# Four of eleven down groups of an FP4 feed-forward layer: exact codes in two passes and a rescale on VectorE, in place of three passes

## The reference

```python
def _dequant_fp4(packed_i32, scales_f16, group_size):      # 8 codes in a word, one scale for 128 inputs of one output
    vals = _FP4_LUT[nib.astype(jnp.int32)].reshape(out_f, in_p * 8)
    s_full = jnp.repeat(scales_f16.astype(jnp.float32).T, group_size, axis=1)
    return vals * s_full
w_gu = _dequant_fp4(gate_up_packed, gate_up_scales, GROUP_SIZE)     # 2816 x 512
w_down = _dequant_fp4(down_packed, down_scales, GROUP_SIZE)         # 512 x 1408: 11 groups of 128 inputs
gate, up = (gate_up[..., :I], gate_up[..., I:])                     # gate_up = x @ w_gu.T, I = 1408
h = jax.nn.silu(gate) * up
y = jnp.einsum('bsi,hi->bsh', h, w_down)
rms = jnp.sqrt(jnp.mean(y * y, axis=-1, keepdims=True) + EPS)
return y / rms
x = _layernorm(x + _L0_ffn_ref(x, ...), axis=-1)                    # the last of three such lines
```

## Time and profile before

| | |
|---|---|
| runs | 532.00, 533.84, 530.71 us; median 532.0 us |
| the profiled execution | 532.28 us, its span 530.6 us |
| busy share of the span: PE, ACT, POOL, DVE | 95%, 75%, 72%, 70% |
| matmuls | 3612 |
| mean granted clock of TensorE | 0.988 |
| DMA | 40.6 MB, 77 GB/s |

### The profile page before, as it was taken

One profiled execution on the slowest core, in us unless ns is written; L12 is line 12 of the kernel. 1 busy time (PEld: TensorE's weight loads), 2 busy tenths in 40 slices (PEclk: granted clock), 3 DMA queues, 4 the chain that ended last, 5 costly groups with the idle time before them and its releaser, 6 DMA issues.

```text
span 530.6 us, 11816 instructions
## 1 busy us (share of the span) xinstructions
PE 504.4 (95%) x3612; PEld 372.5 (70%) x3612; DVE 370.9 (70%) x1161; ACT 400.5 (75%) x962; POOL 383.6 (72%) x449
## 2 busy tenths in 40 slices
PE   8998986999999999999999999999999999999992
PEld 6776775668876677667766776777677667776651
DVE  2876665898887677867777787778686876674223
ACT  4478864046999988878877887888689868978981
POOL 2576883696899499959976996799679968972231
PEclk9999998999999999999999999999999999999997
DMA  8443766325026666313213320322041102001001
GB/s 230 138 100 82 167 142 134 79 56 140 12 61 132 156 111 150 71 48 115 56 24 86 86 62 4 114 64 59 0 119 40 40 1 80 2 2 40 1 21 40
DMA packets 98786, 40.63 MB, mean 77 GB/s; under 512 B 72570, under 2 KB 90106, under 8 KB 98746
## 3 DMA queue, kind: packets, MB, share of 16 engines
q1 hardware_dynamic: 98746, 40.14, 31.1%
HBM read 27.46 MB, written 12.66 MB: 76 GB/s over the span
## 4 chain that ended last, share of the span: by engine, by line
PE 67%; POOL 7%; issue 7%; SPq 6%; ACT 5%; DVE 3%; DMA 3%; POOLq 0%; DVEq 0%; ACTq 0%
PE p_cv L129 6%; PE p_cv L131 6%; PE p_cv L130 6%; PE p_n L1284 5%; PE p_n L1283 5%; PE p_n L1282 5%; SPq L401 5%; PE p_qk L1269 4%; PE p_x L1269 4%; PE p_x L1271 4%; PE p_qk L1271 4%; PE p_qk L882 3%; PE p_s L1269 3%; PE p_s L1271 3%; POOL shared L283 2%
## 5 line engine op out<-in xcount | busy, mean ns | idle before, releaser
L1120 ACT ACTIVATE p_qk<-p_qk,rescale 128x256 f32<-128x256 f32 x192 | 79.8, 464 | 24.6 <-PE p_qk L1271 24.2
L129 PE MATMUL p_cv<-kv_hi,toe 128*128 128x288 f16 x320 | 92.6, 289 | 5.9 <-DMA toe<-toeplitz_rows 4.5
L1088 POOL TENSOR_TENSOR h_lo<-w,h_hi 128x256 f16<-128x256 f32 x88 | 68.9, 795 | 35.6 <-ACT h_hi L1137 35.5
L130 PE MATMUL p_cv<-kv_lo,toe 128*128 128x288 f16 x320 | 92.5, 289 | 0.0
L131 PE MATMUL p_cv<-kv_hi,toe 128*128 128x288 f16 x320 | 92.5, 289 | 0.0
L283 POOL TENSOR_TENSOR shared<-shared 128x1024 f32<-128x1024 f32 x32 | 75.6, 2362 | 11.5 <-DVE shared L243 11.4
L1120 ACT ACTIVATE p_x<-p_x,rescale 128x256 f32<-128x256 f32 x192 | 79.8, 468 | 0.8
L1282 PE MATMUL p_n<-wd_hi,h_hi 128*128 128x512 f16 x176 | 66.7, 379 | 0.0
L1283 PE MATMUL p_n<-wd_lo,h_hi 128*128 128x512 f16 x176 | 66.7, 379 | 0.0
L1284 PE MATMUL p_n<-wd_hi,h_lo 128*128 128x512 f16 x176 | 66.7, 379 | 0.0
L1269 PE MATMUL p_qk<-x_hi,wg_hi 128*128 128x256 f16 x256 | 63.0, 273 | 2.4 <-DVE w L1183 1.5
(11 more groups left out here) (167 smaller groups left out, 1237.3 us busy)
## 6 DMA issues: line engine op xcount, KB each, us to landing
toe<-toeplitz_rows SPq DMA_DIRECT2D x16, 512.0 KB, 3.7
cnat<-in_ctx SPq DMA_DIRECT2D x128, 32.0 KB, 2.0
xq<-x_blocks SPq DMA_DIRECT2D x16, 256.0 KB, 5.6
xr<-x_rows SPq DMA_DIRECT2D x16, 256.0 KB
out_x<-fin SPq DMA_DIRECT2D x16, 256.0 KB
ring<-in_x SPq DMA_DIRECT2D x6, 512.0 KB, 4.1
x_rows<-ring SPq DMA_DIRECT2D x6, 512.0 KB, 3.9
x_blocks<-ring SPq DMA_DIRECT2D x48, 64.0 KB
```

Source lines behind the costliest of these rows:

```text
L129: nc.tensor.matmul(dst, hi, kh, start=(mb == 0), stop=False)
L130: nc.tensor.matmul(dst, hi, kl, start=False, stop=False)
L1088: nc.gpsimd.tensor_tensor(h_lo[:, i, :], h32[:, i % 2, :], h_hi[:, i, :], ALU.subtract).then_inc(h_low, 1)
L1120: done = nc.scalar.activation(sums, sums, ACT.Copy, scale=rescale[:, p - 1, part * GI + i:part * GI + i + 1])
```

## The change

Groups 0 to 3 of the down weights (`EX = 4`) are kept as their FP4 codes without scales. The codes are exact in f16, so these groups have no low half: `wd_lo` holds seven groups, and their `y` steps are two matmuls. The scales come back on the sum: after group i (0 to 2) VectorE multiplies the whole PSUM sum of the half by scale(i)/scale(i+1), after group 3 by scale(3) (steps `s0_<i>`, `s1_<i>`, in the last body `S1_<i>`, line 1235). Group i+1 waits for that. In the first stage the ratios are worked out on VectorE (`dr`), written to HBM (`rw`) and loaded on all partitions (`rl`, 128 x 2048); four weight tiles are copied in place of scaled, transposed once in place of four times, and have no `wl`. Some early tiles share one buffer with the ratios. All tables of steps are new.

```diff
-                if kind == "g":
+                if kind == "g" or idx < EX:
...
+            elif name == "rl":
+                sp.wait_ge(ratios_stored, 16)
+                sp.wait_ge(scales_flipped, 2)
+                sp.wait_ge(unpacked, 30)
+                sp.wait_ge(rows_stored, 16)
+                sp.dma_start(early[:, 0:EX * D].rearrange("p (g d) -> p g d", g=EX), bass.AP(ratio_rows.tensor, 0, [[0, P], [D, EX], [1, D]])).then_inc(
+                    keep["in_ratio"], 16)
...
-            for g in range(1 if n < OG else 4):
+            for g in range(1 if n < OG + EX else 4):
...
+        def down_ratios():
+
+            dve.wait_ge(in_dr, 16)
+            nc.vector.tensor_scalar(dn_abs[:], dn_rows[:], FP4_SHIFT, None, ALU.mult).then_inc(ratios_made, 1)
...
+            nc.vector.reciprocal(dn_rec[:, 1:EX], dn_abs[:, 1:EX]).then_inc(ratios_made, 1)
+            dve.wait_ge(ratios_made, 4)
+            nc.vector.tensor_tensor(dn_abs[:, 0:EX - 1], dn_abs[:, 0:EX - 1], dn_rec[:, 1:EX], ALU.mult).then_inc(
+                ratios_made, 1)
...
+        def rescale_down(f, t, i):
+            dve.wait_ge(y_part[t], f * EX + i + 1)
+            if isinstance(f, int) and f == 0 and t == 0 and i == 0:
+                dve.wait_ge(keep["in_ratio"], 16)
+            nc.vector.tensor_tensor(p_y[t][:], p_y[t][:], keep["early"][:, i * D:(i + 1) * D], ALU.mult).then_inc(y_rescaled[t], 1)
...
-            nc.tensor.matmul(p_y[t][:], h_hi[:, i, c], wd_hi[:, i, :], start=(i == 0), stop=False)
-            nc.tensor.matmul(p_y[t][:], h_hi[:, i, c], wd_lo[:, i, :], start=False, stop=False)
-            done = nc.tensor.matmul(p_y[t][:], h_lo[:, i, c], wd_hi[:, i, :], start=False, stop=(i == GI - 1))
-            if i == GI - 1:
+            if 0 < i <= EX:
+                pe.wait_ge(y_rescaled[t], f * EX + i)
+            nc.tensor.matmul(p_y[t][:], h_hi[:, i, c], wd_hi[:, i, :], start=(i == 0), stop=False,
+                             skip_group_check=True)
+            if i >= EX:
+                nc.tensor.matmul(p_y[t][:], h_hi[:, i, c], wd_lo[:, i - EX, :], start=False, stop=False,
+                                 skip_group_check=True)
+            done = nc.tensor.matmul(p_y[t][:], h_lo[:, i, c], wd_hi[:, i, :], start=False,
+                                    stop=(i < EX or i == GI - 1), skip_group_check=True)
+            if i < EX:
+                done.then_inc(y_part[t], 1)
...
-    PE_ORDER = ("y1_0 g0_0 g1_0 g2_0 y1_1 y1_2 y1_3 y1_4 g0_1 g1_1 g2_1 y1_5 y1_6 g0_2 g1_2 c2 g0_3 g2_2 c3 "
...
+    PE_ORDER = ("g0_0 g1_0 y1_0 g2_0 g0_1 g1_1 g2_1 g0_2 g1_2 g2_2 y1_1 g0_3 c2 g1_3 c3 g2_3 g3_0 g4_0 y1_2 "
...
```

More of the change, by code:

```diff
@@ L39 @@
 RING = 5
+EX = 4
 LATE = ("y1", "n1", "a1", "b1", "e1")
@@ L1020, in periods @@
         "y_done", "y_squared", "y_used", "rr_made", "rs3_made", "fin_made", "y_steps"))
+    y_part, y_rescaled = ([sem(f"{n}{t}") for t in range(GT)] for n in ("y_part", "y_rescaled"))
     def before(i):
@@ L1240, in body @@
                     low_x2(g, int(s[2]))
+                elif s[0] in "sS":
+                    rescale_down(f - 1 if s[:2] == "s1" else f, int(s[1]), int(s[3:]))
                 else:
@@ L1321, in decoder_layer @@
     x1_blocks = nc.dram_tensor("x1_blocks", [2 * NG, 4, P, P], F32, kind="Internal").ap()
-    START_SYNC = ("x4 tw0 cx2 cx3 cx0 cx1 x3 cx4 toe1 st0 x5 st1 st2 x6 st3 xq0 toe0 xr1 cx6 cx7 xq1 xr0 cx5 "
-                  "x7 toe2 xq2 cx8 xr2 cx10 cx11 xq3 cx9 toe3 xq4 xr3 cx14 cx12 toe4 toe5 cx13 st4 cx15 xq5 "
-                  "st5 st7 st6").split()
-    START_PE = ("ze0 Xa0 iw0 iw1 Xb0 iw2 iw3 iz0 Q0 V0 Xa1 S0 w0 Xb1 M0 N0 Q1 T0 Oa0 w1 w2 Ob0 S1 w3 Xa2 V1 "
[9 rows of a table removed]
-                "+xt1 +y0_10 +d1").split()
@@ L1385, in decoder_layer @@
-    LAST_POOL = "hl0 hl1 hl2 hl3 a1 hl4 hl5 hl6 hl7 b1 hl8 hl9 hl10 A1 a0 B1 b0".split()
+    ratio_rows = nc.dram_tensor("ratio_rows", [EX, D], F32, kind="Internal").ap()
+    START_SYNC = ("x3 cx0 cx1 tw0 x4 cx2 cx3 toe0 st0 x5 st1 st2 x6 st3 cx4 xq0 xq1 xr0 xq2 rw0 cx6 rl0 toe1 "
+                  "cx7 x7 toe2 xr1 xq3 cx5 cx10 cx8 cx9 toe3 toe4 cx11 xq5 xr2 xq4 toe5 cx12 xr3 cx13 st4 "
+                  "st5 cx14 cx15 st6 st7").split()
+    START_PE = ("ze0 iw0 Xa0 iw1 Xb0 iz0 iw2 iw3 Q0 V0 Xa1 S0 M0 Xb1 N0 Q1 T0 w0 w1 Oa0 Ob0 Xa2 w2 V1 S1 w3 "
[9 rows of a table added]
+                "+xt1 +d0 +d1").split()
@@ new lines, in decoder_layer @@
+    POOL_ORDER = ("pr1 pr2 hl0 tr0 pr3 hl1 hl2 tr1 hl3 pn hl4 hl5 tr2 a1 tr3 hl6 bn0 hl7 b1 hl8 hl9 bn1 hl10 "
+                  "a0 b0").split()
+    LAST_PE = ("g0_0 g1_0 g2_0 y1_0 g0_1 g1_1 g2_1 g0_2 y1_1 g1_2 g2_2 y1_2 g0_3 g1_3 y1_3 g2_3 g3_0 g4_0 "
[3 rows of a table added]
+               "y0_5 y0_6 y0_7 y0_8 y0_9 y0_10").split()
+    LAST_DVE = ("s1_0 s1_1 s1_2 gu0 gu1 s1_3 gu2 gu3 gu4 a1 s0_0 b1 gu5 S1_0 s0_1 gu6 gu7 s0_2 S1_1 s0_3 "
+                "S1_2 S1_3 e1 gu8 gu9 gu10 A1 B1 E1 a0 b0 e0").split()
+    LAST_ACT = ("tl rs0_1 rs1_1 rs2_1 rs0_2 rs1_2 rs2_2 rs0_3 rs1_3 rs2_3 gu0 gu1 hh0 hh1 gu2 rs3_1 rs4_1 "
+                "ho0 rs5_1 rs3_2 hh2 rs4_2 rs5_2 rs3_3 rs4_3 rs5_3 gu3 gu4 hh3 hh4 n1 rs6_1 rs7_1 rs6_2 "
+                "rs7_2 gu5 rs6_3 rs7_3 hh5 gu6 gu7 rs8_1 hh6 rs9_1 rs10_1 rs8_2 rs9_2 rs10_2 rs8_3 hh7 rs9_3 "
+                "rs10_3 gu8 gu9 hh8 gu10 hh9 hh10 ho1 N1 n0").split()
```

102 lines of the change are left out of this document (62 added, 40 removed), and 60 rows, old and new, of tables (LAST_PE, PE_ORDER, START_ACT, START_DVE).

## The result

The changed kernel took 540.51 us (median of 5 runs, 536.91 to 540.78) where the kernel before took 531.11 in the same comparison: ratio 1.0135, 95% interval 1.0104 to 1.0167. The forecast was 527 us. The profiled execution is the one of 536.91 us, span 534.5, against 532.28 and 530.6 before. So two things have to be explained: 3.9 us between the two profiles, and some 3.5 us by which most executions of the changed kernel are longer than the profiled one.

What follows compares the result with a forecast made beforehand. TensorE was taken to bound a full body. First stage -4.6, six bodies -0.6, last body +0.2 made -5.0 us on the profiled 532.28, so 527.3, median 527.0; own range 523 to 530, wider range 521 to 535.

Steps and rivals of the forecast that it cites:

- The first stage (-4.5 - 0.87 + 0.75): First stage: earlier convolutions -4.5 us, four matmuls fewer in body 1 -0.87, wait into body 2 +0.75; sum -4.6.
- GpSimd's sums, which lead on to the feed-forward layer: First stage: GpSimd's sums, beginning at 97.61, were said to lead on to the feed-forward layer without a gap.
- Without a fall of the clock behind them: First convolutions: c2 and followers run from about 89.3 instead of 92.6, with no clock fall behind; gain 4.5 us.
- upper bound of 5.4: First stage: largest gain allowed for the earlier convolutions, 5.4 us, if the clock stays up all through; lower bound 0.
- The opening (1.1 a body): Opening of six bodies and the last: TensorE waits 1.1 us each for ScalarE's rescales of the gate sums.
- The boundary (0.63): Five boundaries from body 2 to 7: TensorE idle 0.63 us each ahead of g0_0, for VectorE's low half of xt1.
- Into the last body 1.73: Boundary into the last body: no d0 and d1 to fill the time, so TensorE waits 1.73 us.
- the bound that I gave: Bodies behind g0_3: waits like those of before, so 0, with 0.4 us a body to either side.
- The rescale (0.68 us): VectorE, eight whole-bank rescales a body: 0.68 us each, 5.4 us a body, mostly hidden while VectorE has gaps.
- Rival 3: Bodies: VectorE becomes the bound, at 1.0 us a rescale, +2 us a body, 539 us; chance 0.20.
- The rule on shared ports: Output step fin, VectorE sharing ports with GpSimd: boundary wait might grow 0.4 us, 2 us in sum, giving 529; not adopted.
- Rival 2: First stage: toe1 lands late behind 1 MB of ratios, ninth convolution gives the gain back; no change, 531.5 us; chance 0.25.

Runs made afterwards that it cites:

- run 12: Kernel before the change, loads toe0 and toe1 exchanged and load x7 directly behind toe1: 529.26 us, ratio 0.9951.
- C: The changed kernel itself, against the kernel before: 540.51 us, ratio 1.0135; measured again without edit, 539.0 us, ratio 1.0140.
- run 8: C with the 64 rescale multiplications on VectorE replaced by semaphore increments, waits and order kept: 539.38 us, ratio 1.0130.
- run 6: C with load toe1 early and toe0 behind xq0, as before the change: 540.76 us, ratio 1.0142.
- run 7: C with VectorE's first-stage step dn6 (denominators, reciprocal, coef) two products earlier: 535.19 us, ratio 1.0052.
- run 5: Kernel before the change with only the loads toe0 and toe1 exchanged: 533.65 us, ratio 1.0024.
- run 2: C with VectorE's last low weight tile and kl1 ahead of the transpose of xq0 in the first stage: 537.62 us, ratio 1.0124.
- run 3: C with VectorE's low half of xt1 ahead of e1 and a0, as before the change: 537.02 us, ratio 1.0108.
- run 4: C with TensorE's y1_0 ahead of g0_0, y1_1 and y1_2 between the gate parts, in the six full bodies: 570.75 us, ratio 1.0744.
- run 10: C with ScalarE's gate rescales cut to 16 of 256 columns for gate columns 0 to 2, result left wrong: 533.05 us, ratio 1.0009.
- run 11: C with VectorE's kq0, kq1, low half of xt1 and s1_1 earlier, and TensorE's y1 steps moved into the opening: 548.46 us, ratio 1.0286.

## Why the prediction was wrong, point by point

- **The first stage (-4.5 - 0.87 + 0.75) is the step that failed.** "I work out the fourth product at 93.0 against 97.5": it came at about 94, with xq0 a microsecond later than before, so the gain of the start was real, 3.5 us at the first sum. What failed is what the sum left out. It took only the start of the convolutions and put VectorE's new order behind it at nothing, without a reason. The stretch from the first sum to g0_0 of body 1 shows what that order costs:

| trace | first sum (us) | g0_0 of body 1 | between |
|---|---|---|---|
| before | 97.61 | 131.59 | 33.98 |
| before, run 12 | 93.57 | 127.61 | 34.04 |
| C | 94.12 | 132.75 | 38.63 |
| C's order, clock fallen (run 8) | 96.41 | 135.07 | 38.66 |
| C with toe0 late (run 6) | 98.75 | 137.40 | 38.65 |
| C with dn6 moved (run 7) | 96.01 | 130.76 | 34.75 |

  Within one order the stretch does not depend on when it starts, so a gain at the start is carried to its end, as the forecast assumed, unless a load comes too late for it (x7 in run 5, the context in run 2). C's order makes the stretch 4.65 us longer. VectorE leads it there, and its steps that meet GpSimd last 4.7 us more than before; run 7, which moves the step at one of the two costliest meetings, takes 3.9 us of the 4.65 back. The last 0.8 us stay open.
- **"GpSimd's sums, which lead on to the feed-forward layer"** was a misreading. GpSimd is busy there nearly all the time, but the chain of before runs through TensorE, and that of C through VectorE.
- **"Without a fall of the clock behind them"** holds for two profiled executions of C. In six other traces with C's order up to there (runs 3, 4, 7, 8, 10 and 11) the clock fell; in run 8 that cost 2.3 us. The forecast itself left a wait of TensorE in that place (c2 from 89.3) and should have priced the fall behind it; its upper bound of 5.4, "if the clock stays up", does not fit a 4.5 that already stands without a fall. That the other executions of C at 539 to 541 us are the same is inferred from those traces and from their clocks (0.987 to 0.993 against 0.993 to 0.996); none of them has a trace.
- **The opening (1.1 a body)** was right: 1.2, and run 10 shows that it is ScalarE's pace.
- **The boundary (0.63)** was right in its cause and too small: 0.98, of which 0.40 stands ahead of g0_0 (run 3 takes just that) and the rest at d1, y0_10 and xt1. Into the last body 1.73 was 1.72. With these, a full body came out 0.4 longer than forecast, the edge of the bound that I gave.
- **The rescale (0.68 us)** was right at 0.691, and at nothing for the bodies too (run 8). Rival 3, "VectorE becomes the bound", gave nearly the right time, 539, for a wrong reason: what made VectorE decide was its order, in the first stage and at the boundary of the bodies; in the bodies run 8 rules out its load.
- **The rule on shared ports** was weighed at the output step of the bodies, at 2 us, and left out. It belonged in the first stage, where two-operand steps of VectorE lie beside GpSimd's long sums.
- **Rival 2** (toe1 late behind the ratios) did not occur: c8 followed without such a wait.

## What to carry to other kernels

A gain at the start of a stage is one term, and what the new order makes of the rest of the stage is another: price both. Ask which engine leads the rest in the new order, and read that engine's long instructions beside its neighbour's. To tell the two terms apart, measure the stretch behind the gain on its own, in several traces with different starts. Work that used to fill another engine's wait stops being a filler when it is itself made to depend on a third one. And where two engines share a resource, the same two orders of steps can differ by microseconds by who comes first at a meeting; look for durations of one form that differ by a factor, and for ends that coincide.

## What was not expected of the hardware

A VectorE step of 128x4 took 2.00 us where it takes 0.16 alone, held to the end of a GpSimd sum of 2.36 us. Whether the clock falls at the gap ahead of the first convolution is not settled by the length of the gap alone: it stayed at 1.00 behind 2.88 and 2.79 us of idle TensorE in two profiles of C, and fell to 0.50 behind 2.73 us in run 3 (88 to 90 us), whose order is C's up to there.
